# A graph convolution and mixture-of-experts kernel on one core: gather groups of eight, four and two blocks, and another order of the last stage

## The chip, the core and the metric

The kernel runs on one core of a Trainium2 chip, as one launch. The metric is the device time of that launch in microseconds (us). Engines are called by their short names: PE (TensorE), ACT (ScalarE), DVE (VectorE), POOL (GpSimd) and SP (SyncE, which only issues transfers here).

## What is computed

The input is x with 1250 rows of 1024, and 40000 edges, each with a source row, a target row and one of 8 types. Cut to what matters:

```python
xn = layernorm(x)
out = xn @ root + bias
for r in range(8):                       # mean over the edges of type r that end in a row
    sums = segment_sum(xn[src] * (type == r), dst);  cnt = segment_sum(type == r, dst)
    out += (sums / max(cnt, 1)) @ weight[r]
z = concat([out, xn]) @ w_gate + b_gate
x = x + tanh(out) * z + xn * (1 - z)
t = layernorm(x)                         # two of eight experts (1024 -> 512 -> 1024, relu) a row
x = x + layernorm(t + sum of the two experts' outputs, weighted) * gamma + beta
```

## The kernel before, in words

**Precision.** Every matmul operand is split in a rounded high part (made by ACT) and the rest, a low part (made by DVE); a product of 128 x 1024 by 1024 x 512 is three times eight matmuls. Weights come in chunks of four pieces of 128 x 1024: SP loads a piece (`load_piece`, L180), ACT makes its high part (`hi_piece`, L196), DVE its low part (`lo_piece`, L202). A raw buffer holds two pieces, so piece 2 of a chunk is only loaded when piece 0 has been split.

**Chunk stage.** The rows are first multiplied with all eight relation weights (16 chunks, ten row tiles each; PE line L211), and the products are stored in `y_dram`. One tile of one chunk is called a step here. Beside it, in chunks 1 to 3, the edges are sorted by target tile. Edge columns are taken four at a time (a batch, 79 in all): `hots` on DVE writes two one-hot tiles (L702, L705) into one of eight slots, and `counts` on PE multiplies them (L617), three batches at the end of each step, one step after the step in which DVE's list has them. PE waits there for `hot_ready`; DVE waits for `hot_used` of the batch eight before. The same DVE queue holds, at steps given in the table `side`, `starts` (where each tile's edges begin, L725 to L770), `positions` for ten tiles (L774 to L780: three tiles in step 2 of chunk 2, three in step 6, two in steps 0 and 2 of chunk 3), then `records`; and `lo_piece` in steps 2, 4, 6 and 8 of each chunk. Later POOL scatters 313 columns of records into the sorted list.

**Gather stage.** The sorted list has 332 blocks of 128 edges. For each block POOL gathers 128 rows of `y_dram` (512 KB) by an indirect DMA into one of eight slots (L982), ACT scales them into `y_hi`, which has two slots (L1030), DVE makes the low part (L1069), and PE adds both through a one-hot matrix into two PSUM banks: two matmuls for the high part (L1108), two for the low (L1115). ACT also makes the one-hot matrix (L993, L1002). Blocks that end in the same tile of target rows form a group: 78 groups of four and 10 groups of two. After each group DVE adds the two banks to `acc` (`flush`, L1051); it does so behind the low parts of the next group, and PE waits for the flush of the group two before. Two groups make a pass, 44 in all, numbered from 0. In each pass but four PE also works one unit, 24 matmuls of the products with root (the first 20 units, added to `acc` by DVE, also L1051) and with the gate weights (the next 20, copied by ACT, L1020); between the two matmul pairs of a block stand three of them. Passes 8, 19, 30 and 41 have no unit: in them the next chunk's four pieces are split, one ahead of each block, and their groups are short (two blocks each), as are those of pass 43. The pieces go into the buffer that the units before them read, so ACT waits for the last of these.

**Last stage.** Experts' outputs are scattered with addition into `sum_dram`. When the last is in, POOL adds `sum_dram` to `acc` by ten accumulating DMAs (L1710, one a tile). The tiles are normalised in groups (0 to 2, 3 to 5, 6 and 7, 8 and 9; L1832 to L1848 on DVE, L1786 on ACT). POOL adds tiles 0 to 7 to `out` by accumulating DMAs (L1714); for tiles 8 and 9 DVE adds rows that were loaded before (L1852) and SP stores them plainly (L1677).

## Time and profile before

| | us |
|---|---|
| median of 3 runs | 2188.13 |
| lowest and highest run | 2180.44, 2189.11 |
| the profiled execution | 2187.53 |
| its span in the trace | 2185.7 |
| chunk stage with the sort, about | 88 to 950 |
| gather stage | 960 to 1568 |
| last DMA landings | 2182 |

The terms are set against the profiled execution's 2187.53 us, which is 0.6 us under the median. Lines (L702) are those of the kernel before. The trace gives the start and the duration of each instruction; consecutive instructions of one engine can overlap by a little, so the distance of two starts is less than a duration where nothing lies between. Where the text says that a pass takes so long, it is from the first L1030 of its blocks to the first of the next pass.

### The profile page before, as it was taken

What the parts mean: (1) busy time and instruction counts of PE and PEld (TensorE: products, weight loads), DVE (VectorE), ACT (ScalarE), POOL (GpSimd) and SP (SyncE); (2) the same over time, 40 slices, a digit from 0 to 9 for tenths busy, and PEclk for the clock granted to TensorE, in tenths of its full rate; (3) what the DMA queues carried; (4) which work ended last, traced back from release to release, by engine and by line L of the source; (5) the groups of instructions that cost most, each with busy time, mean ns of one, the idle gap of its engine ahead of it and who ended that gap; (6) DMA issues with size and microseconds to landing.
All of it is one profiled execution on the core that took longest, in us unless ns stands there. A gap on an engine that the chain in (4) does not pass through costs nothing. (4 is left out here: it accounts for less than half of the span.)

```text
span 2185.7 us, 28064 instructions
## 1 busy us (share of the span) xinstructions
PE 2011.1 (92%) x9425; PEld 1596.2 (73%) x9425; DVE 1284.4 (59%) x2282; ACT 969.2 (44%) x1506; POOL 904.0 (41%) x801
## 2 busy tenths in 40 slices
PE   8999999999999999999899899899799579899970
PEld 6777778778888888877677577677488468788860
DVE  8589588832222222139899899899798742222215
ACT  3211122222222222249899799899644223233332
POOL 0000046565655555237677588688200022212212
PEclk9999999999999999999899899999799779999995
DMA  5224487777777877679889799899565579998439
GB/s 185 100 81 134 137 272 247 259 251 253 254 258 259 256 258 256 227 223 321 273 292 315 242 329 319 272 331 313 194 178 176 199 266 326 305 318 287 103 75 188
DMA packets 156848, 520.96 MB, mean 238 GB/s; under 512 B 30748, under 2 KB 31132, under 8 KB 154672
## 3 DMA queue, kind: packets, MB, share of 16 engines
q1 hardware_dynamic: 85616, 310.51, 41.1%
q0 software_dynamic: 71104, 208.84, 32.1%
q8 instruction: 68, 1.11, 0.2%
q14 instruction: 60, 0.49, 0.1%
HBM read 383.83 MB, written 154.68 MB: 246 GB/s over the span
## 5 line engine op out<-in xcount | busy, mean ns | idle before, releaser
L211 PE MATMUL psum<-w_hi,xnT_hi 128*128 128x512 f32 (+1 forms) x1592 | 421.1, 399 | 4.6 <-PEq L228 2.5
L211 PE MATMUL psum<-w_lo,xnT_hi 128*128 128x512 f32 (+1 forms) x1592 | 417.8, 393 | 0.0
L211 PE MATMUL psum<-w_hi,xnT_lo 128*128 128x512 f32 (+1 forms) x1592 | 413.7, 394 | 0.0
L882 POOL DMA_INDIRECT sorted_rows<-acc x313 | 342.9, 1096 | 116.7 <-issue 85.3
L580 ACT ACTIVATE work<-psum 128x512 f32<-128x512 f32 (+1 forms) x150 | 89.7, 598 | 661.5 <-PE psum L211 661.5
L211 PEld LDWEIGHTS psum<-w_hi,xnT_hi 128*128 128x128 f32 (+1 forms) x1592 | 293.5, 187 | 75.4 <-issue 4.0
L211 PEld LDWEIGHTS psum<-w_lo,xnT_hi 128*128 128x128 f32 (+1 forms) x1592 | 294.9, 185 | 73.2
L211 PEld LDWEIGHTS psum<-w_hi,xnT_lo 128*128 128x128 f32 (+1 forms) x1592 | 294.3, 185 | 71.1
L982 POOL DMA_INDIRECT w_hi<-y_rows,sort_row x168 | 221.2, 1317 | 78.3 <-PE psum L1115 41.3
L982 POOL DMA_INDIRECT w_lo<-y_rows,sort_row x164 | 217.9, 1329 | 77.2 <-PE psum L1115 38.6
L1108 PE MATMUL psum<-y_hi,hot 128*128 128x512 f32 x664 | 220.0, 414 | 30.2 <-ACT y_hi L1030 27.4
L1069 DVE SCALAR_TENSOR_TENSOR w_hi<-w_hi,sort_recip,y_hi 128x1024 fp32r<-128x1024 f32 x168 | 213.0, 1282 | 24.0 <-ACT y_hi L1030 19.0
L202 DVE TENSOR_TENSOR w_lo<-w_raw,w_hi 128x1024 fp32r<-128x1024 f32 x86 | 105.1, 1223 | 207.4 <-ACT w_hi L196 207.0
L1069 DVE SCALAR_TENSOR_TENSOR w_lo<-w_lo,sort_recip,y_hi 128x1024 fp32r<-128x1024 f32 x164 | 207.9, 1282 | 14.3 <-ACT y_hi L1030 9.1
L850 DVE TENSOR_TENSOR acc<-acc 128x1024 fp32r<-128x1024 f32 x64 | 78.4, 1225 | 220.0 <-ACT acc L589 220.0
L1030 ACT ACTIVATE y_hi<-w_hi,sort_recip 128x1024 fp32r<-128x1024 f32 x168 | 192.0, 1143 | 18.7 <-DVE w_hi L1069 8.5
L1030 ACT ACTIVATE y_hi<-w_lo,sort_recip 128x1024 fp32r<-128x1024 f32 x164 | 187.3, 1142 | 12.5 <-DVE w_lo L1069 8.7
L1108 PEld LDWEIGHTS psum<-y_hi,hot 128*128 128x128 f32 x664 | 124.9, 195 | 74.1 <-issue 35.3
L879 POOL TENSOR_TENSOR gate_word<-gate_word 1x1 f32<-1x1 f32 x40 | 8.4, 211 | 348.4 <-DVE acc L818 201.8
L1694 POOL DMA_INDIRECT sum_rows<-o_s,row_at x27 | 42.9, 1589 | 262.7 <-DMA sum_rows<-o_s,row_at 124.9
L993 ACT ACTIVATE apart<-lanes,sort_local 128x128 f16<-128x128 f32 x332 | 127.2, 386 | 6.1 <-DVE lanes L1044 6.1
L1051 DVE TENSOR_TENSOR acc<-acc,psum 128x1024 f32 (+2 forms) x108 | 120.6, 1117 | 2.5 <-DVE acc L1051 0.4
(334 smaller groups left out, 2614.0 us busy)
## 6 DMA issues: line engine op xcount, KB each, us to landing
split_experts<-acc SPq DMA_DIRECT2D x128, 512.0 KB, 4.2
ring<-split_experts SPq DMA_DIRECT2D x16, 4096.0 KB, 16.1
w_raw<-in_wchunks SPq DMA_DIRECT2D x86, 512.0 KB, 5.0
y_rows<-work SPq DMA_DIRECT2D x144, 256.0 KB, 2.8
acc<-in_wchunks SPq DMA_DIRECT2D x64, 512.0 KB, 6.0
work<-local_rows SPq DMA_DIRECT2D x26, 384.0 KB, 4.2
sum_rows<-work SPq DMA_DIRECT2D x22, 256.0 KB, 4.5
acc<-in_bias SPq DMA_DIRECT2D x10, 512.0 KB, 5.5
```

The costliest lines, as they stand in the source:

```text
L202: v.tensor_tensor(w_lo[:, s, q * PIECE:(q + 1) * PIECE], raw_piece(c, q), w_hi[:, s, q * PIECE:(q + 1) * PIECE].bitcast(F32), ALU.subtract)\
L211: i = pe.matmul(to[:rm, :], x_[:, k, m * P:m * P + rm], w_[:, s, k * HALF:(k + 1) * HALF], start=(n == 0), stop=(n == 3 * KD - 1))
L580: act.activation(stage_y[:rows(m), t % 4, :], bank[t % 4][:rows(m), :], ACT.Copy)\
L850: v.tensor_tensor(x_lo[:, p % 2, :], x_raw[:, p % 2, :], x_hi[:, p % 2, :].bitcast(F32), ALU.subtract).then_inc(x_lo_done, 1)
L882: pool.indirect_dma_start(sorted_dram, IndirectOffsetOnAxis(ap=e_dest[:, c:c + 1], axis=0), e_rec[:, c, :], None, bounds_check=BLOCKS * P ...
L982: pool.indirect_dma_start(slot_of(b).bitcast(F32), None, y_dram, IndirectOffsetOnAxis(ap=sort_row[:, COLUMN[j]:COLUMN[j] + 1], axis=0), bo ...
L993: act.activation(apart[:, k, :], lanes[:, :], ACT.Square, bias=sort_local[:, at:at + 1], scale=-1.0)\
L1030: act.activation(y_hi[:, j % 2, :], slot_of(b).bitcast(F32), ACT.Copy, scale=sort_recip[:, COLUMN[j]:COLUMN[j] + 1]).then_inc(hi_done, 1)
L1051: v.tensor_tensor(at, at, of, ALU.add).then_inc(acc_done, 1)
L1069: v.scalar_tensor_tensor(out=slot_of(b), in0=slot_of(b).bitcast(F32), scalar=sort_recip[:, COLUMN[j]:COLUMN[j] + 1], in1=y_hi[:, j % 2, :] ...
L1108: o = pe.matmul(bank[2 * h + q], hot[:, h, k, :], y_hi[:, j % 2, q * HALF:(q + 1) * HALF], start=first, stop=False)
L1694: pool.indirect_dma_start(sum_dram, IndirectOffsetOnAxis(ap=row_at[:, b:b + 1], axis=0), o_s[:, b % 2, :], None, compute_op=ALU.add).then_ ...
```

## The change

The list of groups has three kinds now: 34 groups of eight blocks (`LONG`), 10 of four and 10 of two, again 332 blocks. A group of eight fills both halves of a pass and one pair of banks, and is flushed once; the flushes fall from 88 to 54. Passes 8, 19, 30 and 41 have eight blocks; pieces 0 and 1 are split there ahead of the second block, piece 2 ahead of the seventh, piece 3 ahead of the eighth. Short passes (two and two blocks) are now 5, 11, 22, 33 and 43, passes with two groups of four are 4, 10, 21, 32 and 39; in a short pass with a unit six matmuls of it stand at each block.

In the sort, `starts` loses what comes behind the running sums; this goes into `shifts` (chunk 1, step 8) and `owners` (chunk 3, step 8). `positions` has one tile in each step from step 1 of chunk 2 to step 0 of chunk 3, and two more operations over 313 columns a tile.

In the last stage the order of tile groups is 8 and 9 first; SP loads their sums plainly into the ring of expert weights, DVE adds them, and DVE's last additions for these tiles stand behind the statistics of tiles 0 to 2. The core of the diff:

```diff
-SHORT = GROUP // 2
-SHORT_GROUPS = TILES
-LONG_GROUPS = -(-((EDGES + TILES * (SHORT * P - 1)) // (SHORT * P) - SHORT_GROUPS) // 4) * 2
-GROUPS = LONG_GROUPS + SHORT_GROUPS
+LONG, SHORT = 2 * GROUP, GROUP // 2
+SIDE_GROUPS = 2 * TILES
+LONG_GROUPS = -(-((EDGES + TILES * (SHORT * P - 1)) // (SHORT * P) - 3 * TILES) // 4)
+GROUPS = LONG_GROUPS + SIDE_GROUPS
+QUADS = 2 * LONG_GROUPS + SIDE_GROUPS
...
                     for t in range(1, TILES):
+                        v.tensor_tensor(t_mid_start[:, t:t + 1], t_mid_start[:, t - 1:t], t_mid[:, t - 1:t], ALU.add)
...
+                def shifts():
+                def owners():
...
                 def positions(first, last):
...
-                        link(v.tensor_scalar(e_tail, e_scan, t_tail[:, t:t + 1], t_shift[:, t:t + 1], ALU.is_gt, ALU.mult))
+                        v.tensor_scalar(e_tail, e_scan, t_mid_at[:, t:t + 1], t_mid_shift[:, t:t + 1], ALU.is_gt, ALU.mult)
+                        link(v.tensor_scalar(e_last, e_scan, t_odd_at[:, t:t + 1], t_odd_shift[:, t:t + 1], ALU.is_gt, ALU.mult))
                         link(v.tensor_tensor(e_scan, e_scan, e_tail, ALU.add))
+                        link(v.tensor_tensor(e_scan, e_scan, e_last, ALU.add))
...
-                side = {(HIST_CHUNK, 3): [turned], (HIST_CHUNK, 5): [starts],
-                        (HIST_CHUNK + 1, 2): [lambda: positions(0, 3)], (HIST_CHUNK + 1, 6): [lambda: positions(3, 6)],
-                        (HIST_CHUNK + 2, 0): [lambda: positions(6, 8)], (HIST_CHUNK + 2, 2): [lambda: positions(8, TILES)],
-                        (HIST_CHUNK + 2, 4): [records], (LOOK_CHUNK, 0): [table]}
+                side = {(HIST_CHUNK, 3): [turned], (HIST_CHUNK, 5): [starts], (HIST_CHUNK, 8): [shifts],
+                        (HIST_CHUNK + 2, 4): [records], (HIST_CHUNK + 2, 8): [owners], (LOOK_CHUNK, 0): [table]}
+                for t in range(TILES):
+                    side[(HIST_CHUNK + 1 + (t + 1) // TILES, (t + 1) % TILES)] = [lambda t=t: positions(t, t + 1)]
...
-        SHORT_PASSES = (*PIECES_AT, PASSES - 1)
+        SHORT_PASSES = (*(i + 3 for i in PIECES_AT if i + 3 < PASSES), TILES // 2, PASSES - 1)
+        MID_PASSES = (*(i - 1 for i in SHORT_PASSES[:-1]), PASSES - 5)
+        KIND = [SHORT if i in SHORT_PASSES else GROUP if i in MID_PASSES else LONG for i in range(PASSES)]
...
+        PIECES_BEFORE = {1: (0, 1), 6: (2,), 7: (3,)}
...
-                        if g >= 1:
+                        if g >= 1 and ENDS[g - 1]:
                             flush(g - 1)
...
-                        if g >= 2:
-                            pe.wait_ge(acc_done, ACC_NO[g - 2])
+                        if BEGINS[g] and PAIR[g] >= 2:
+                            pe.wait_ge(acc_done, ACC_NO[PAIR[g] - 2])
...
-                            for _ in itertools.islice(steps, 3 * KD // SLOTS):
+                            for _ in itertools.islice(steps, 3 * KD // (FIRST[2 * i + 2] - FIRST[2 * i])):
...
-            TAIL_GROUPS = ((0, 3), (3, 6), (6, 8), (8, 10))
+            TAIL_GROUPS = ((8, 10), (0, 3), (3, 6), (6, 8))
...
+                sp.wait_ge(o_added, 16 * BLOCKS_T)
+                for m in LAST_TILES:
+                    sp.dma_start(sum_here(m), sum_dram[m * P:m * P + rows(m), :]).then_inc(o_got[m], 16)
...
-                for m in range(TILES):
+                for m in range(LAST_TILES[0]):
                     pool.dma_start(acc[:rows(m), m, :], sum_dram[m * P:m * P + rows(m), :], accum_op=ALU.add)\
                         .then_inc(o_got[m], 16)
...
+                        if m in LAST_TILES:
+                            link(v.tensor_tensor(acc[:rm, m, :], acc[:rm, m, :], sum_here(m), ALU.add))
```

## Rows read from the trace of the kernel before

**Rows 1.** The page: span, and busy time of each engine.
```profile
span 2185.7 us, 28064 instructions
PE 2011.1 (92%) x9425; PEld 1596.2 (73%) x9425; DVE 1284.4 (59%) x2282; ACT 969.2 (44%) x1506; POOL 904.0 (41%) x801
```

**Rows 2.** Groups of DVE, 142.1 to 264.1: busy us, mean ns | idle before, releaser.
```profile
L702 DVE TENSOR_TENSOR acc<-acc 128x320 f16<-128x320 f32 (+1 forms) x53 | 25.5, 480 | 8.3 <-PE psum L617 8.1
L777 DVE TENSOR_TENSOR acc<-acc 128x313 f32<-128x313 f32 x10 | 4.9, 487 | 0.3
L776 DVE TENSOR_SCALAR acc<-acc 128x313 f32<-128x313 f32 x10 | 4.4, 442 | 0.4
```

**Rows 3.** Timeline in chunk 2: start, us, engine, line, [idle before <- releaser].
```profile
148.36 0.49 DVE L702 TENSOR_TENSOR acc<-acc 128x320 f16<-128x320 f32 x1 [3.01 <-PE psum L617]
148.77 0.69 DVE L705 TENSOR_TENSOR acc<-acc 128x512 f16<-128x512 f32 x1
...
160.21 0.63 PE L617 MATMUL psum<-acc 128*128 128x80 f16 x12
...
162.08 0.32 DVE L774 TENSOR_SCALAR acc<-acc 128x313 f32<-128x313 f32 x1
...
165.38 1.23 DVE L202 TENSOR_TENSOR w_lo<-w_raw,w_hi 128x1024 fp32r<-128x1024 f32 x1
166.52 0.48 DVE L702 TENSOR_TENSOR acc<-acc 128x320 f16<-128x320 f32 x1
...
167.53 0.48 DVE L702 TENSOR_TENSOR acc<-acc 128x320 f16<-128x320 f32 x1
```

**Rows 4.** Busy time by engine, ten steps of chunk 3 (columns as in rows 5).
```profile
203.10:264.10 61.00, 61.00 (x362) 48.12 (x359) 42.96 (x85) 9.78 (x15) 0.00 (x0) 1.00 0.39 125
```

**Rows 5.** Busy time: passes 12-16, 24-28, then 7-9, 18-20, 29-31, 40-42.
```profile
core 0: us, PE busy (x) PEld busy (x) DVE busy (x) ACT busy (x) POOL busy (x), PEclk, DMA share, GB/s
1132.40:1199.40 67.00, 65.98 (x281) 52.20 (x281) 64.41 (x56) 61.38 (x91) 51.57 (x40) 1.00 0.90 315
1299.10:1365.00 65.90, 65.90 (x282) 51.49 (x281) 61.42 (x51) 63.25 (x97) 53.64 (x41) 1.00 0.91 324
1061.10:1106.10 45.00, 37.30 (x129) 25.50 (x129) 38.25 (x34) 35.01 (x52) 28.17 (x22) 0.81 0.75 245
1212.80:1259.50 46.70, 37.65 (x129) 25.85 (x129) 38.38 (x34) 35.01 (x51) 26.54 (x20) 0.78 0.69 227
1365.00:1407.40 42.40, 34.07 (x129) 23.40 (x128) 36.41 (x31) 35.39 (x53) 26.12 (x20) 0.88 0.77 254
1513.30:1556.00 42.70, 32.85 (x107) 19.72 (x105) 35.67 (x31) 34.47 (x51) 25.45 (x19) 0.80 0.84 278
```

**Rows 6.** Timeline of DVE in pass 21: a flush and four low parts.
```profile
1266.89 1.22 DVE L1051 TENSOR_TENSOR acc<-acc,psum 128x1024 f32 x1
...
1268.03 5.21 DVE L1069 SCALAR_TENSOR_TENSOR w_lo<-w_lo,sort_recip,y_hi 128x1024 fp32r<-128x1024 f32 x4
```

**Rows 7.** The chain that ended last, one piece: 24 matmuls back to back.
```profile
1952.55 5.49 PE psum L1875 x24
```

**Rows 8.** Groups, 1212.8 to 1259.5 (passes 18 to 20).
```profile
L1108 PE MATMUL psum<-y_hi,hot 128*128 128x512 f32 x40 | 15.2, 465 | 7.7 <-ACT y_hi L1030 7.4 <-issue 0.2
L196 ACT ACTIVATE w_hi<-w_raw 128x1024 fp32r<-128x1024 f32 x4 | 4.2, 1054 | 8.0 <-DMA w_raw<-in_wchunks 5.6 <-PE psum L211 2.4
```

**Rows 9.** DMA, 2131 to 2183: busy tenths in 40 slices; queues: packets, MB, share.
```profile
DMA  7999999999999999999999999999999999998420
q0 software_dynamic: 2576, 9.32, 93.3%
q1 hardware_dynamic: 256, 0.93, 4.6%
```

**Rows 10.** Timeline of the end: POOL's last store, DVE's last addition.
```profile
2165.10 0.85 POOL L1714 DMA_DIRECT2D out<-acc  x1 [0.19 <-issue]
...
2171.39 1.22 DVE L1852 TENSOR_TENSOR acc<-acc,w_raw 98x1024 f32<-98x1024 f32 x1
```

More of the change, by code:

```diff
@@ L54 @@
 SLOTS = 8
-PASSES = GROUPS // 2
+PASSES = QUADS // 2
 UNITS = 4 * TILES
@@ L900, in program @@
                      4 * TILES + 1: CH_GATEU}
-        SHORT_PASSES = (*PIECES_AT, PASSES - 1)
-        ORDER, FIRST, COLUMN = [], [0], []
+        SHORT_PASSES = (*(i + 3 for i in PIECES_AT if i + 3 < PASSES), TILES // 2, PASSES - 1)
+        MID_PASSES = (*(i - 1 for i in SHORT_PASSES[:-1]), PASSES - 5)
+        assert not {*SHORT_PASSES, *MID_PASSES} & {*PIECES_AT}
+        KIND = [SHORT if i in SHORT_PASSES else GROUP if i in MID_PASSES else LONG for i in range(PASSES)]
+        BASE = {LONG: 0, GROUP: LONG_GROUPS * LONG, SHORT: LONG_GROUPS * LONG + TILES * GROUP}
+        NUMBER = {LONG: 0, GROUP: LONG_GROUPS, SHORT: LONG_GROUPS + TILES}
+        taken = {kind: 0 for kind in BASE}
+        OWNER, BEGINS, ENDS, PAIR, FIRST, COLUMN, pair = [], [], [], [], [0], [], -1
         for i in range(PASSES):
             for h in range(2):
-                short = i in SHORT_PASSES
-                n = sum((g >= LONG_GROUPS) == short for g in ORDER)
-                at, size = (LONG_GROUPS * GROUP + n * SHORT, SHORT) if short else (n * GROUP, GROUP)
-                ORDER.append(LONG_GROUPS + n if short else n)
-                COLUMN += range(at, at + size)
+                kind = KIND[i]
+                begins, ends = kind < LONG or h == 0, kind < LONG or h == 1
+                n, part = taken[kind], h * GROUP if kind == LONG else 0
+                pair += begins
+                OWNER.append(NUMBER[kind] + n)
+                BEGINS.append(begins)
+                ENDS.append(ends)
+                PAIR.append(pair)
+                at = BASE[kind] + n * kind + part
+                COLUMN += range(at, at + min(kind, GROUP))
                 FIRST.append(len(COLUMN))
+                taken[kind] += ends
         assert sorted(COLUMN) == list(range(BLOCKS))
@@ L916, in size_of, with pieces_in @@
             return FIRST[g + 1] - FIRST[g]
-        def pieces_in(i):
-            return [(PIECES_AT[i], q) for q in range(PIECES)] if i in PIECES_AT else []
+        PIECES_BEFORE = {1: (0, 1), 6: (2,), 7: (3,)}
+        def pieces_in(i, n=None):
+            if i not in PIECES_AT:
+                return []
+            return [(PIECES_AT[i], q) for q in (range(PIECES) if n is None else PIECES_BEFORE.get(n, ()))]
         def ended_before(i):
@@ L1021, in _ @@
                                         .then_inc(zx_read, 1)
-                        if pieces:
-                            c, q = pieces[n]
+                        for c, q in pieces_in(i, n):
                             act.wait_ge(mm_done, c * TILES)
@@ L1065, in _ @@
                             b = j % SLOTS
-                            if pieces:
-                                lo_piece(v, pieces[j - FIRST[2 * i]][0], 0, pieces[j - FIRST[2 * i]][1])
+                            for c, q in pieces_in(i, j - FIRST[2 * i]):
+                                lo_piece(v, c, 0, q)
                             v.wait_ge(hi_done, j + 1)
@@ L1114, in _ @@
                             for q in range(2):
-                                o = pe.matmul(bank[2 * h + q], hot[:, h, k, :], slot_of(b)[:, q * HALF:(q + 1) * HALF],
+                                o = pe.matmul(bank[two + q], hot[:, h, k, :], slot_of(b)[:, q * HALF:(q + 1) * HALF],
                                               start=False, stop=last)
@@ L1638, in program, with sum_here @@
             GOT = [p + 16 * len(range(i, BLOCKS, SLOTS)) for i, p in enumerate(PLACED)] + [0, 0]
-            TAIL_GROUPS = ((0, 3), (3, 6), (6, 8), (8, 10))
+            TAIL_GROUPS = ((8, 10), (0, 3), (3, 6), (6, 8))
+            TAIL_ORDER = [m for lo, hi in TAIL_GROUPS for m in range(lo, hi)]
             block = stage.enter_context(nc.Block())
             LAST = BLOCKS_T - 1
-            LAST_TILES = range(*TAIL_GROUPS[-1])
+            LAST_TILES = range(*TAIL_GROUPS[0])
             y_ready = ssem("f_y")
+            def sum_here(m):
+                return ring[:, 0, 0, 0, (m - LAST_TILES[0]) * D:(m - LAST_TILES[0] + 1) * D][:rows(m), :].bitcast(F32)
             def x1_rows(m):
@@ L1836, in _ @@
                         v.wait_ge(const_in, 16 * (1 + len(LAST_TILES)))
+                    if g == 1:
+                        for m in LAST_TILES:
+                            v.wait_ge(scaled, TAIL_ORDER.index(m) + 1)
+                            o = acc[:rows(m), m, :]
+                            v.tensor_tensor(o, o, x1_rows(m), ALU.add).then_inc(y_ready, 1)
                     s, std, r, w = var_of[:, lo:hi], std_of[:, lo:hi], recip_of[:, lo:hi], w_of[:, lo:hi]
```

113 lines of the change are left out of this document (69 added, 44 removed).

## The prediction

> **What bounds the kernel now.** I began with the page: PE is busy for 92% of the span and no other engine for over 59% [rows 1], so a change off PE pays only where PE waits for it, and costs only where it makes PE wait. The change touches three stages, and for each I asked for what ends last there.
>
> In the chunk stage PE does not pause at all: ten steps take 61.0 us, all of them PE's [rows 4], 6.1 a step. DVE has slack, but not much. It runs ahead in the one-hot batches until the eight slots stop it: it idles 3.01 us for PE's counts, then ends the third batch of a step at 149.46, and PE takes it at 160.5, in the burst from 160.21 [rows 3]. So DVE's lead is at most 11.0 us, and what it must do beyond 6.1 us a step is drawn from that.
>
> In the gather stage a pass takes 13.40 us in the root half and 13.18 in the gate half [rows 5]. In the first, DVE sets it: low parts are 1.30 apart and a flush takes 1.14 from start to start [rows 6]; eight of one, two of the other and one addition of a unit (0.72) make 13.4. In the second, PE is busy throughout [rows 5]. Its floor is 56 matmuls at 0.229 [rows 7], 12.8 us. The trios of passes around the four splittings are the poor stretches: 45.0, 46.7, 42.4 and 42.7 us, 176.8 in all, for 20 blocks each, at a mean clock of 0.78 to 0.88 [rows 5]. In one of them ACT waited 8.0 us ahead of the pieces, 5.6 for their loads and 2.4 for PE, and PE 7.7 for ACT [rows 8]. DMA engines are 90% busy in plain passes [rows 5].
>
> In the last stage the DMA engines are full from 2132 to 2178 [rows 9].
>
> **Chunk stage: `starts`, `positions`, `owners`.** A tile's positions take 3.30 us (162.08 to 165.38), a batch 1.01, a low piece 1.14 [rows 3]. Added to a tile are one comparison, 0.442 long and with nothing to wait for, so some 0.40, and one addition, 0.487 and a wait of 0.03 [rows 2]: 0.92, a tile 4.22. A step with one tile costs DVE 3.03 + 4.22 = 7.25 against PE's 6.1, so 1.13 is drawn ten times (11.3), and 1.14 for each of four low pieces (4.6): 15.9 against a lead of 11.0. **PE is starved for 4.9 us**, in the last three or four of these steps. The old order drew 9.9 + 1.14 + 3.03 - 6.1 = 8.0 at once for three tiles, and let the lead come back before the next three. Bounds: nothing, if the lead is full later than I think; 20, if PE's clock falls meanwhile (below). Of the rest, `starts` becomes shorter; `shifts`, a dozen small operations, falls where the lead can return; `owners`, some 46 of about 0.2, takes 9 us behind the last batches, where DVE idles 18 of 61 us [rows 4]: nothing. POOL and SP move no transfer here; the scatters start later by what PE loses.
>
> Weighed against the trace: a batch's two operations last 0.48 and 0.69 but the next batch starts 1.01 after [rows 3], so they overlap by 0.15. The Trainium skill ("VectorE: DVE Perf Modes", "The DRAIN you can't avoid") says that the next operation does not start until the pipeline has emptied; by that the batches cost 1.17, and the sum below would be worse by the 4.9 us that the second rival works out. The row decides; the rule is kept as that rival.
>
> **Gather stage, plain passes.** 34 flushes of 1.14 go, 39 us of DVE, but PE's floor catches most. Root half: DVE falls to 12.3, PE sets the pass with 12.8 and small waits, I take 12.97: 0.43 off each of nine passes (2, 3, 6, 12 to 17), 3.9. Gate half: 13.18 to 13.0 in eleven passes (23 to 28, 34 to 38), 2.0. Bounds: nothing, and 0.6 and 0.38 a pass at the bare floor. The second pass, where DVE still catches up, gives 0.5. Passes of two groups of four stay as they are.
>
> **Short passes with a unit.** Passes 5, 11, 22 and 33 have 40 matmuls, 9.2 us at the floor, I take 9.4, where plain passes stood: 4.0 off twice and 3.8 twice, **15.6 off**. This is no gain yet: the four blocks taken out stand in the splitting passes.
>
> **Splitting passes, now eight blocks.** ACT gives PE one more block before it waits, and five blocks lie between pieces 1 and 2 in which these land, so most of the 8.0 of wait is filled. What is late next is DMA: eight gathers and four pieces, twelve times 0.524 MB, 6.3 MB; at the 324 GB/s and 0.91 of [rows 5] the engines give 356 full, so 17.7 us. DVE has 8 x 1.30 + 4 x 1.14 + 1.14 = 16.1 and some waits. I take 18.2, and 18.8 with the gate half's stores. The pass ahead takes 12.97 or 13.0; the one behind 13.2 and 1.5 for a low clock (bounds 0 and 6), in the third region 14.0 in all, and 12.2 behind the last, which has no unit. The trios: 45.9, 45.9, 45.8 and 44.0, together 181.6 against 176.8, **4.8 more**, for 24 blocks each instead of 20. Bounds: 10 less to 8 more.
>
> Gather stage in all: 3.9 + 2.0 + 0.5 + 15.6 - 4.8 = **17.2 off**, bounds 5 and 30. Waits for the flush two groups back go, and none comes in their place: a flush now stands half a pass behind its group.
>
> **Last stage.** POOL's queue took 93.3% of 52 us for 9.32 MB, 5.2 us a MB; SP's 4.6% for 0.93 MB, 2.6 a MB [rows 9]. Two tiles (0.93 MB) that go from accumulating to plain save 2.4 us of a full resource. Against it, DVE has two additions of 1.22 more [rows 10], and the accumulating stores, which cost most, now end the kernel: for tiles 6 and 7 they were issued by 2165.1, 6 us ahead of DVE's last addition [rows 10], and now are last in DVE's order. I take **1.5 off**, bounds 2.4 off and 3 more. The Trainium skill ("DMA: Bandwidth & Descriptors", "Issuing engines are not separate DMA queues") says that another issuing engine saves only the time of issue; by that alone the move would give under 1 us. The rows above price the accumulation, not the issuer.
>
> **Sum.** 2187.5 + 4.9 - 17.2 - 1.5 = 2173.7; the profiled execution lies 0.6 under the median, so **2174 us**. About 0.5%, 11 us, is what a measurement of this kernel can tell from no change; the border to faster lies at 2177.
>
> **Rivals.**
> 1. *PE's clock falls when DVE starves it in chunk 2 and 3* (slower). In the trios PE's pauses came with a mean clock of 0.78 to 0.88 [rows 5]. A step's 24 matmuls at 1.2 GHz instead of 2.4 cost 5.5 more. Over four starved steps 22, which takes the place of the 4.9: 2174 + 17 = 2191. It decides from the point where over three steps run low; five give 2196, six over 2199. For it: DVE stays the slower engine in these steps, so pauses repeat. Against it: a slow PE lets DVE catch up, which ends the pauses. Chance 0.13.
> 2. *DVE's operations cost their full durations*: batches 1.17, so 0.48 more a step over ten steps, 4.9 more, 2179. Against it, [rows 3]. Chance 0.07.
> 3. *Transfers bind the gather stage.* Passes stay at 13.4 and 13.18 because landings come later, and the splitting passes take 20: 5.9 and 8 less gain, partly made up in the passes behind: 2184. For it, 0.90 and 0.91 [rows 5]; against it, a plain pass would need only 0.94 of the engines. Chance 0.18.
> 4. *No starvation*: 2169. Chance 0.08.
>
> **How the numbers follow.** The forecast has 0.54, from 2166 to 2182 by its own terms, 0.44 of it faster and 0.10 the same. Rival 1 gives 0.08 slower and 0.05 the same; rival 2 mostly the same (0.06); rival 3 0.15 the same, 0.01 faster, 0.02 slower; rival 4 faster. The rest of rival 2 is faster. That makes 0.54 faster, 0.36 the same, 0.10 slower. The range reaches from the low end of rival 4 to rival 1's value: 2161 to 2190.
>
> **What would show it.** In the changed trace: waits of L617's line for DVE's one-hot tiles of some 5 us, in the last steps of chunk 2 and the first of chunk 3, clock at 1.00 there; 54 full flushes; plain passes of 12.9 to 13.0 with DVE under 95%; short passes of 9.4; splitting passes of 18 to 19 with ACT's wait for pieces under 2 us each; the last landing 1 to 2 us nearer to the last scatter. The prediction is wrong if PE never waits in the chunk stage or waits over 10 us, if plain passes do not shorten, or if the trios cost over 190 us.

## The result and the profile after

The kernel after takes 2175.53 us in the median of 8 runs (2168.59 to 2178.73), the kernel before 2188.73 beside it (8 runs, 2180.44 to 2194.39): a ratio of 0.9943, interval 0.9926 to 0.9960. That is 13.2 us faster by the medians and 12.5 us by the ratio. The forecast was 2174. Medians hide how it came about, so the profiled execution (2178.36 us, span 2176.6) is cut where stages meet, beside before's and a later execution of the same kernel after (e10):

| us | before | after | e10 |
|---|---|---|---|
| start to the first block scaled (L1030, after L1080) | 966.0 | 977.5 | 975.3 |
| gather stage, to the last block scaled | 595.9 | 569.7 | 572.5 |
| to the landing of the last scatter into `sum_dram` | 567.2 | 572.9 | 567.9 |
| to the kernel's last landing | 52.9 | 52.9 | 51.6 |
| to the end of the span | 3.7 | 3.6 | 3.6 |

The page after, with what answers to [rows 1]:

```profile
span 2176.6 us, 27961 instructions
PE 2012.9 (92%) x9425; PEld 1601.7 (74%) x9425; DVE 1263.6 (58%) x2307; ACT 970.8 (45%) x1506; POOL 913.2 (42%) x799
```

PE is as busy as before in a span 9.1 us shorter: nothing was taken from its work.

**Chunk stage.** The groups of DVE from 149.9 to 279.5 answer to [rows 2]; L810 and L811 are the comparisons, L812 and L813 the additions:

```profile
L706 DVE TENSOR_TENSOR acc<-acc 128x320 f16<-128x320 f32 (+1 forms) x50 | 24.0, 480 | 6.9 <-PE psum L621 6.7
L812 DVE TENSOR_TENSOR acc<-acc 128x313 f32<-128x313 f32 x10 | 4.9, 487 | 0.3
L813 DVE TENSOR_TENSOR acc<-acc 128x313 f32<-128x313 f32 x10 | 4.9, 487 | 0.3
L810 DVE TENSOR_SCALAR acc<-acc 128x313 f32<-128x313 f32 x10 | 4.4, 443 | 0.4
L811 DVE TENSOR_SCALAR acc<-acc 128x313 f32<-128x313 f32 x10 | 4.4, 437 | 0.0
```

The timeline where chunk 2 meets chunk 3 answers to [rows 3]:

```profile
203.80 0.48 DVE L706 TENSOR_TENSOR acc<-acc 128x320 f16<-128x320 f32 x1
204.20 0.68 DVE L709 TENSOR_TENSOR acc<-acc 128x512 f16<-128x512 f32 x1
...
204.67 0.63 PE L621 MATMUL psum<-acc 128*128 128x80 f16 x12
204.81 0.32 DVE L808 TENSOR_SCALAR acc<-acc 128x313 f32<-128x313 f32 x1
...
208.46 0.48 DVE L816 TENSOR_TENSOR acc<-acc 128x313 f32<-128x313 f32 x1
208.98 1.23 DVE L203 TENSOR_TENSOR w_lo<-w_raw,w_hi 128x1024 fp32r<-128x1024 f32 x1
...
210.30 3.75 PE L212 MATMUL psum<-w_hi,xnT_hi 128*128 128x512 f32 x8 [5.00 <-issue]
```

The seventh tile's positions are done, and the eighth's (L808 to L816) begin. PE ends its 12 counting matmuls at 205.3 and stands still until 210.30. It waits for the last low piece of chunk 3's weights (L203), which is in DVE's queue behind these positions. The wait is called "issue" because the releaser is not resolved; the low piece ends at 210.21 and PE starts 0.09 later. The eight matmuls behind it take 3.75 us. The windows, with the columns of [rows 5], show the clock:

```profile
203.10:209.30 6.20, 2.20 (x20) 1.43 (x18) 5.96 (x13) 0.60 (x1) 0.00 (x0) 1.00 0.00 0
209.30:216.20 6.90, 5.90 (x14) 4.67 (x15) 6.73 (x13) 0.00 (x0) 0.00 (x0) 0.51 0.65 214
```

0.51 is the lower level, 1.2 GHz. From the start of one step's counts to the start of the next, this one step takes 13.96 us instead of 6.11: 5.0 of wait and 2.8 for matmuls at the low clock. All others of chunks 2 and 3 take what they took, so 7.85 of the 11.5 us by which the stage is longer are here (7.5 of 9.3 in e10).

Another 2.3 us lie where the sort's counting has ended and the forecast had nothing. From the fourth step of chunk 4 (283.86 before, 293.05 after) to the first block scaled (966.01, 977.54) it is 682.1 us before and in e1, and 684.2 to 684.6 in all twelve traces of kernels with the new groups: a step of 24 matmuls takes 5.57 us there instead of 5.55, over some 118 steps in which PE hardly pauses. Which part of the program does this was not tested. What is left is mostly in the first 100 us, which differ between executions (the fourth step of chunk 1 starts at 97.6 to 100.9, whatever the kernel).

**Gather stage.** Windows of passes 13 to 17 and 24 to 28, then the trios 7 to 9, 18 to 20, 29 to 31 and 40 to 42 (24 blocks each now, 20 before), against [rows 5]:

```profile
1145.20:1210.10 64.90, 64.90 (x281) 52.49 (x281) 59.09 (x51) 61.81 (x91) 51.67 (x40) 1.00 0.91 323
1288.50:1354.40 65.90, 65.90 (x282) 51.81 (x281) 56.18 (x46) 63.20 (x96) 53.13 (x41) 1.00 0.94 337
1065.70:1110.10 44.40, 37.91 (x146) 26.63 (x145) 40.09 (x35) 41.16 (x60) 35.04 (x26) 0.96 0.93 334
1210.10:1253.30 43.20, 38.08 (x148) 27.04 (x147) 40.02 (x35) 40.54 (x60) 33.54 (x24) 0.96 0.95 344
1354.40:1398.00 43.60, 38.97 (x147) 27.50 (x146) 38.22 (x32) 41.39 (x61) 34.44 (x25) 0.92 0.96 349
1499.20:1541.50 42.30, 35.58 (x125) 22.92 (x123) 38.33 (x33) 40.61 (x60) 34.34 (x24) 0.92 0.97 352
```

A root pass now takes 12.99 and all of it is PE. A gate pass takes 13.18 as before, and a second look at [rows 5] shows why: PE was busy for 65.90 of 65.90 us there too, with 5.2 us of DVE work more. The trios take 173.3 us for 96 blocks, where they took 176.8 for 80, at a mean clock of 0.92 to 0.96 instead of 0.78 to 0.88. In the first splitting pass the groups of ACT and DVE that answer to [rows 8] read:

```profile
L203 DVE TENSOR_TENSOR w_lo<-w_raw,w_hi 128x1024 fp32r<-128x1024 f32 x4 | 4.8, 1223 | 1.4 <-ACT w_hi L197 1.4
L197 ACT ACTIVATE w_hi<-w_raw 128x1024 fp32r<-128x1024 f32 x4 | 4.1, 1056 | 1.5 <-DMA w_raw<-in_wchunks 1.0 <-PE psum L212 0.4
```

ACT's wait ahead of the pieces is 1.5 us, 1.0 of it for loads, where in the same pass before it was 6.3 and 3.9; in passes 19, 30 and 41 it is 0.4, 0.0 and 0.0 ([rows 8] has 8.0 before for pass 19). Windows of the four splitting passes, then the 3.7 us behind the first of them, and the DMA view of the first:

```profile
1078.70:1096.50 17.80, 11.89 (x40) 6.19 (x38) 16.20 (x15) 16.17 (x24) 14.43 (x11) 1.00 0.97 355
1223.20:1240.30 17.10, 12.69 (x40) 7.60 (x38) 16.05 (x15) 16.01 (x23) 12.82 (x9) 0.90 0.95 339
1367.60:1385.10 17.50, 13.48 (x40) 8.34 (x38) 15.59 (x14) 16.72 (x24) 13.89 (x9) 0.80 0.96 343
1512.40:1529.30 16.90, 12.72 (x40) 7.36 (x38) 15.18 (x14) 16.37 (x24) 14.08 (x8) 0.90 0.95 342
1096.50:1100.20 3.70, 3.12 (x7) 2.44 (x8) 3.64 (x4) 3.69 (x6) 2.51 (x2) 0.54 1.02 410
```

```profile
DMA packets 1727, 6.31 MB, mean 355 GB/s; under 512 B 187, under 2 KB 187, under 8 KB 1726
```

They take 17.79, 17.14, 17.51 and 16.95 us, the passes behind them 13.44, 12.97, 12.93 and 12.14 (pass 42 has no unit, nor has 43; with the four that the description names there are six). The low clock has not gone: it holds for 3.4 us right behind the first splitting pass, and for part of each of the others. A short pass and the one behind it take 22.65 (root) and 22.95 (gate) together.

**Last stage.** The last 53 us, before and then after (the first fence is before's):

```profile
2129.10:2182.00 52.90, 0.00 (x0) 0.00 (x0) 32.58 (x66) 11.63 (x14) 15.91 (x18) 0.50 0.96 194
```

```profile
2120.10:2173.00 52.90, 0.00 (x0) 0.00 (x0) 34.92 (x68) 11.62 (x14) 14.03 (x16) 0.50 0.95 194
```

DVE has 2.34 us more, and nothing is gained. What the DMA engines had to do, share of the engines times the stretch, comes to 50.9 us before (91.7% for POOL's 9.32 MB and 4.5% for SP's 0.93 MB) and 50.1 us after (packets, MB, share of the engines):

```profile
q0 software_dynamic: 2304, 8.39, 84.2%
q1 hardware_dynamic: 512, 1.85, 10.5%
```

POOL's stores wait for ACT's scaling of each group of tiles and go out later than they did: the last (2163.72, below) 43.6 us behind the last scatter's landing, where it was 36.0 before. L1902 are DVE's last additions for tiles 8 and 9.

```profile
2138.64 1.22 DVE L1902 TENSOR_TENSOR acc<-acc,t_s 128x1024 f32<-128x1024 f32 x1
2139.78 1.22 DVE L1902 TENSOR_TENSOR acc<-acc,w_raw 98x1024 f32<-98x1024 f32 x1
...
2147.00 0.87 POOL L1773 DMA_DIRECT2D out<-acc  x1 [19.16 <-ACT acc L1845]
...
2156.23 0.84 POOL L1773 DMA_DIRECT2D out<-acc  x1 [6.29 <-ACT acc L1845]
...
2162.68 0.86 POOL L1773 DMA_DIRECT2D out<-acc  x1 [3.53 <-ACT acc L1845]
2163.72 0.84 POOL L1773 DMA_DIRECT2D out<-acc  x1 [0.18 <-issue]
```

### The profile page after: what moved, and what is told of

Same layout as the page of the kernel before. It is cut to its first block and busy times, and to the rows that moved or that the text cites. A ratio compares the mean times of both kernels' runs of the same rounds, so it can differ in the third digit from the quotient of the medians.

```text
span 2176.6 us, 27961 instructions
## 1 busy us (share of the span) xinstructions
PE 2012.9 (92%) x9425; PEld 1601.7 (74%) x9425; DVE 1263.6 (58%) x2307; ACT 970.8 (45%) x1506; POOL 913.2 (42%) x799
## 3 DMA queue, kind: packets, MB, share of 16 engines
q1 hardware_dynamic: 85872, 311.44, 41.3%
## 5 line engine op out<-in xcount | busy, mean ns | idle before, releaser
L1034 POOL DMA_INDIRECT w_hi<-y_rows,sort_row x168 | 230.8, 1374 | 63.2 <-issue 38.0
L1159 PE MATMUL psum<-y_hi,hot 128*128 128x512 f32 x664 | 214.2, 404 | 11.2 <-ACT y_hi L1080 10.6
L203 DVE TENSOR_TENSOR w_lo<-w_raw,w_hi 128x1024 fp32r<-128x1024 f32 x86 | 104.8, 1224 | 189.7 <-ACT w_hi L197 188.8
L1080 ACT ACTIVATE y_hi<-w_hi,sort_recip 128x1024 fp32r<-128x1024 f32 x168 | 192.1, 1144 | 14.7 <-DMA w_hi<-y_rows,sort_row 6.0
L1080 ACT ACTIVATE y_hi<-w_lo,sort_recip 128x1024 fp32r<-128x1024 f32 x164 | 187.6, 1144 | 10.2 <-issue 2.8
L1159 PEld LDWEIGHTS psum<-y_hi,hot 128*128 128x128 f32 x664 | 125.2, 192 | 49.5 <-ACT y_hi L1080 16.2
L1166 PE MATMUL psum<-w_hi,hot 128*128 128x512 f32 x336 | 112.0, 415 | 7.2 <-DVE w_hi L1119 7.1
```

The lines of the kernel that those rows point to most:

```text
L203: v.tensor_tensor(w_lo[:, s, q * PIECE:(q + 1) * PIECE], raw_piece(c, q), w_hi[:, s, q * PIECE:(q + 1) * PIECE].bitcast(F32), ALU.subtract)\
L1034: pool.indirect_dma_start(slot_of(b).bitcast(F32), None, y_dram, IndirectOffsetOnAxis(ap=sort_row[:, COLUMN[j]:COLUMN[j] + 1], axis=0), bo ...
L1080: act.activation(y_hi[:, j % 2, :], slot_of(b).bitcast(F32), ACT.Copy, scale=sort_recip[:, COLUMN[j]:COLUMN[j] + 1]).then_inc(hi_done, 1)
L1159: o = pe.matmul(bank[two + q], hot[:, h, k, :], y_hi[:, j % 2, q * HALF:(q + 1) * HALF], start=first, stop=False)
L1166: o = pe.matmul(bank[two + q], hot[:, h, k, :], slot_of(b)[:, q * HALF:(q + 1) * HALF], start=False, stop=last)
```

## The experiments

All medians; every ratio is to runs of the kernel before on the same chip. "First block" is the first L1080 (L1030), "gather" from there to the last, "last stage" from the last scatter's landing to the last landing of the kernel, all of the profiled execution.

| | median us (runs) | ratio, interval | first block | gather | last stage |
|---|---|---|---|---|---|
| before | 2188.73 (8) | | 966.0 | 595.9 | 52.9 |
| after | 2175.53 (8) | 0.9943, 0.9926 to 0.9960 | 977.5 | 569.7 | 52.9 |
| e1 sort alone | 2196.36 (8) | 1.0041, 1.0025 to 1.0057 | 972.6 | 594.0 | 53.4 |
| e2 sort spread | 2167.19 (6) | 0.9912, 0.9895 to 0.9928 | 967.0 | 570.5 | 51.2 |
| e3 piece first | 2174.35 (6) | 0.9936, 0.9918 to 0.9954 | 974.4 | 574.1 | 54.4 |
| e4 flush length | 2179.43 (11) | 0.9963, 0.9950 to 0.9977 | 975.6 | 576.0 | 52.1 |
| e5 pieces together | 2197.15 (7) | 1.0038, 1.0021 to 1.0056 | 977.1 | 593.4 | 51.1 |
| e6 additions last | 2176.72 (6) | 0.9941, 0.9926 to 0.9955 | 975.0 | 572.3 | 53.9 |
| e7 old last stage | 2172.80 (6) | 0.9932, 0.9909 to 0.9955 | 975.6 | 569.1 | 53.1 |
| e8 spread, additions last | 2164.24 (5) | 0.9887, 0.9870 to 0.9904 | 967.6 | 570.9 | 52.9 |
| e9 groups alone | 2191.06 (12) | 1.0019, 1.0001 to 1.0038 | 975.2 | 591.3 | 51.8 |
| e10 after again | 2172.03 (6) | 0.9943, 0.9921 to 0.9965 | 975.3 | 572.5 | 51.6 |
| e11 spread, old last stage | 2166.70 (6) | 0.9917, 0.9895 to 0.9939 | 968.2 | 571.4 | 53.0 |
| e12 pieces 2 and 3 early | 2199.88 (4) | 1.0062, 1.0042 to 1.0082 | 975.2 | 596.1 | 50.9 |

### What the sort costs, and why

**e1_sort_alone** is the kernel before with the table of steps of the kernel after and two more operations a tile, whose results are not used:

```diff
-                side = {..., (HIST_CHUNK + 1, 2): [lambda: positions(0, 3)], (HIST_CHUNK + 1, 6): [lambda: positions(3, 6)],
-                        (HIST_CHUNK + 2, 0): [lambda: positions(6, 8)], (HIST_CHUNK + 2, 2): [lambda: positions(8, TILES)], ...}
+                for t in range(TILES):
+                    side[(HIST_CHUNK + 1 + (t + 1) // TILES, (t + 1) % TILES)] = [lambda t=t: positions(t, t + 1)]
...
+                        link(v.tensor_scalar(e_last, e_scan, t_tail[:, t:t + 1], t_shift[:, t:t + 1], ALU.is_gt, ALU.mult))
...
+                        link(v.tensor_tensor(e_last, e_last, e_tail, ALU.add))
```

> The kernel before with one part of the change: positions for one tile in each step from chunk 2 step 1 on, and two more DVE operations a tile (their results are not used). Gather and last stage stay as before. Theory A (at the start of chunk 3 PE waits for the last low weight piece, which stands in DVE's queue behind the positions; PE then runs its first matmuls at half clock): one step of about 14 us instead of 6.1, total 8 us above before, about 2197. Theory B (the prediction's: PE is starved for one-hot tiles in three or four steps): 5 us above, 2194, spread over steps, with the waits at the count matmuls. Theory C (the sort costs nothing, the 8 us of the changed trace come from elsewhere): 2189.

Measured: 9.1 us above before, and the same long step, here of 14.02 us:

```profile
205.92 1.22 DVE L202 TENSOR_TENSOR w_lo<-w_raw,w_hi 128x1024 fp32r<-128x1024 f32 x1
...
207.25 3.75 PE L211 MATMUL psum<-w_hi,xnT_hi 128*128 128x512 f32 x8 [5.03 <-issue]
```

The sort's new place and length, without any of the groups, make the long step. The slower plain steps are not in e1: its first block is scaled 6.6 us later than before's, with 7.9 more in the long step.

**e2_spread** is the kernel after with the tiles' positions drawn out, over steps counted from the first of chunk 1 (`records` goes to step 6 of chunk 3):

```diff
-                for t in range(TILES):
-                    side[(HIST_CHUNK + 1 + (t + 1) // TILES, (t + 1) % TILES)] = [lambda t=t: positions(t, t + 1)]
+                for t, at in enumerate((10, 11, 12, 13, 15, 17, 19, 21, 23, 25)):
+                    side[(HIST_CHUNK + at // TILES, at % TILES)] = [lambda t=t: positions(t, t + 1)]
```

> The changed kernel with the ten positions spread over steps 0, 1, 2, 3, 5, 7 and 9 of chunk 2 and 1, 3, 5 of chunk 3, and the records in step 6 of chunk 3: every step with positions is followed by one that lets DVE's lead return, and none stands ahead of the last low piece of chunk 3. Theories A and B: no step over 6.2 us, lead never under 5 us, 8 us below the changed kernel, about 2167.5. Theory C: no difference, 2175.5. If the scatters, which start later by two steps' records at most, were on the path, it would come back there: 2175.

Measured: 2167.19. No step there is over 6.12 us, and the stretch of the long step is full:

```profile
205.00:227.00 22.00, 22.00 (x135) 17.51 (x134) 20.57 (x41) 3.31 (x6) 0.00 (x0) 1.00 0.33 106
```

The same work on DVE costs nothing when its lead is never used up.

**e3_piece_first** puts that low piece ahead of the positions in the one step where it was late:

```diff
+                            if (c, m) == (HIST_CHUNK + 1, 8):
+                                lo_piece(v, c + 1, 1 - s, m // 2 - 1)
                             for of in side.get((c, m), ()):
                                 of()
...
```

> The changed kernel with the last low piece of chunk 3 ahead of the positions in step 8 of chunk 2, nothing else. Theory A alone (only the piece is late): the long step goes from 14 to about 7 us, the others stay at 6.1, 7 us below the changed kernel, 2168.5. Theories A and B together (with the piece out of the way PE next waits for one-hot tiles): the same DVE work is still too much for the lead, three or four steps of 6.5 to 8 us, in all 4 us of wait instead of 8, total 4 us below, 2171.5.

Measured: 2174.35. The long step is gone and four steps of 7.14 to 7.32 us stand in its place, 4.4 us in all, with one-hot tiles late as the prediction had them:

```profile
205.12 1.22 DVE L203 TENSOR_TENSOR w_lo<-w_raw,w_hi 128x1024 fp32r<-128x1024 f32 x1
...
206.44 2.10 PE L212 MATMUL psum<-w_hi,xnT_hi 128*128 128x512 f32 x8 [0.86 <-issue]
...
213.60 0.32 PE L621 MATMUL psum<-acc 128*128 128x80 f16 x4 [0.68 <-DVE acc L709]
```

```profile
205.10:233.90 28.80, 25.62 (x148) 19.74 (x145) 28.07 (x55) 3.33 (x5) 0.00 (x0) 1.00 0.31 104
```

PE pauses for 3.2 of these 28.8 us at a clock of 1.00. The median can't be told from that of the kernel after; the trace can: 3.4 us less in steps there.

### Where the gather stage's gain comes from

**e4_flush_length** gives DVE two linked multiplications that write a scratch tile, about 1.15 us, behind the low parts of each group of eight, where the kernel before had the flush of its first four blocks:

```diff
                         if g >= 1 and ENDS[g - 1]:
                             flush(g - 1)
+                        elif g >= 1:
+                            v.wait_ge(pe_done, FIRST[g])
+                            for _ in range(2):
+                                link(v.tensor_tensor(idle, ..., ALU.mult))
```

> The changed kernel with DVE work of a flush's length (about 1.15 us, on a scratch tile, after the same wait as a flush) where the old kernel had the flushes that now are gone; PE does not wait for it. Theory A (fewer flushes gain through DVE's time in the root half and little in the gate half): root passes back from 13.0 to 13.4, gate passes unchanged at 13.2, the passes that split pieces, where DVE is 91% busy, up by 1.1 each: 9 times 0.4 and 4.5, about 8 us above the changed kernel, 2183.5. Theory B (the gain came from PE no longer waiting for banks, not from DVE's time): under 2 us above, 2177.

Measured: 2179.43; the gather stage is 6.3 us longer (3.5 than in e10). Passes 13 to 17 and 24 to 28:

```profile
1144.70:1211.10 66.40, 66.30 (x282) 52.18 (x281) 63.87 (x61) 61.33 (x91) 50.81 (x40) 1.00 0.91 317
1291.20:1357.10 65.90, 65.90 (x282) 51.75 (x281) 61.46 (x56) 63.13 (x96) 49.37 (x40) 1.00 0.95 338
```

Root passes rise by 0.29 us (of the 0.41 that they had lost), gate passes not at all, so DVE's time counts only where DVE had set the pass. Most of the 26 us must have another source.

**e9_groups_alone** has the new groups in the old places: the splitting passes are short again, with a piece ahead of each of their four blocks.

```diff
-        SHORT_PASSES = (*(i + 3 for i in PIECES_AT if i + 3 < PASSES), TILES // 2, PASSES - 1)
-        MID_PASSES = (*(i - 1 for i in SHORT_PASSES[:-1]), PASSES - 5)
+        SHORT_PASSES = (*PIECES_AT, PASSES - 1)
+        MID_PASSES = (4, 10, 21, 32, 39)
...
-        PIECES_BEFORE = {1: (0, 1), 6: (2,), 7: (3,)}
+        PIECES_BEFORE = {0: (0,), 1: (1,), 2: (2,), 3: (3,)}
```

> The kernel after with groups of eight, four and two, but the places of the kernel before: passes 8, 19, 30 and 41 are short again (four blocks, one piece ahead of each), so no short pass has a unit except the last; passes 4, 10, 21, 32 and 39 have groups of four. Theory A (fewer flushes are worth only what the root passes lose, 0.41 us each, as e4_flush_length said; the rest of the gather stage's 26 us comes from four more blocks beside the pieces): about 13 root passes at 13.0 instead of 13.4 and one at 0.6 less, gate passes at 13.18 as ever, trios at 175 to 177 us for 20 blocks each, the gather stage 589 to 592 us (before 595.9, after 569.7), and the median, which has the sort's 8 to 10 us on it, 2190 to 2196. Theory B (the flushes are the main thing): the gather stage below 580 and the median 2177 to 2183.

Measured: gather 591.3 us, median 2191.06. Fewer flushes alone bring 4.6 of the 26 us; with the sort's cost on top this kernel is not faster than before. Its trios 7 to 9 and 18 to 20 are like those of [rows 5]:

```profile
1068.00:1112.80 44.80, 36.59 (x130) 25.38 (x129) 36.09 (x32) 34.97 (x52) 29.71 (x21) 0.81 0.74 245
1217.10:1262.90 45.80, 35.90 (x130) 24.99 (x129) 36.05 (x32) 34.94 (x52) 27.56 (x20) 0.85 0.70 230
```

**e5_pieces_together** is the kernel after with eight blocks in the splitting passes, but the pieces ahead of the first four; **e12_half_way** leaves pieces 0 and 1 in the place of the kernel after.

```diff
-        PIECES_BEFORE = {1: (0, 1), 6: (2,), 7: (3,)}
+        PIECES_BEFORE = {0: (0,), 1: (1,), 2: (2,), 3: (3,)}      e5
+        PIECES_BEFORE = {1: (0, 1), 2: (2,), 3: (3,)}             e12
```

> The kernel after, with pieces 0, 1, 2 and 3 split ahead of blocks 0, 1, 2 and 3 of passes 8, 19, 30 and 41 instead of ahead of blocks 1, 1, 6 and 7. Theory A (the gather stage owes its gain beyond the shorter DVE queue to the place of the pieces: the load of piece 2, which can only start when piece 0 has been split, lies beside six blocks): ACT waits for the loads of pieces 2 and 3 with nothing else to do, each of the four passes takes 20 to 23 us instead of 17.0 to 17.8, and the median is 12 to 20 us above that of the kernel after (2175.5), about 2191. Theory B (these passes are bound by the bytes they move, 6.3 MB, wherever the pieces stand): the four passes stay at 17 to 18 us and the median at 2175 to 2178.

> The kernel after with pieces 0 and 1 where it has them (ahead of block 1) and pieces 2 and 3 ahead of blocks 2 and 3 instead of 7 and 8. It splits the 22 us that e5_pieces_together lost into the wait of piece 0 for PE's last unit and the wait of pieces 2 and 3 for their loads. Theory A (both count: in e5_pieces_together the pass ahead took 15.85 instead of 13.02, the splitting passes 20.2 to 21.9 instead of 17.0 to 17.8, the pass behind 0.5 to 1 less): the pass ahead is back at 13.0, the splitting passes take 20 to 21 and those behind 12.3, so trios of 45.5 to 47, 183 to 187 us in all (after 173.3), the gather stage about 582 and the median about 2186. Theory B (the loads are all of it): trios of 48 to 49, the gather stage above 590. Theory C (piece 0's wait for PE is all of it): trios of 43 to 44 and a gather stage of 570 to 573.

Measured: 2197.15 and 2199.88, gather stages of 593.4 and 596.1 us. The trios take 195.6 us in e5 (48.3, 48.3, 49.6, 49.3) and 199.1 in e12 (48.7, 49.3, 50.6, 50.4), against 173.3 after. ACT's timelines, first e5:

```profile
1080.66 1.06 ACT L197 ACTIVATE w_hi<-w_raw 128x1024 fp32r<-128x1024 f32 x1 [1.76 <-PE psum L212]
...
1089.53 1.06 ACT L197 ACTIVATE w_hi<-w_raw 128x1024 fp32r<-128x1024 f32 x1 [4.20 <-DMA w_raw<-in_wchunks]
```

then e12:

```profile
1077.94 2.01 ACT L197 ACTIVATE w_hi<-w_raw 128x1024 fp32r<-128x1024 f32 x2 [0.43 <-PE psum L212]
...
1087.82 1.06 ACT L197 ACTIVATE w_hi<-w_raw 128x1024 fp32r<-128x1024 f32 x1 [6.55 <-DMA w_raw<-in_wchunks]
```

and the kernel after:

```profile
1080.55 2.01 ACT L197 ACTIVATE w_hi<-w_raw 128x1024 fp32r<-128x1024 f32 x2 [0.43 <-PE psum L212]
...
1090.85 1.06 ACT L197 ACTIVATE w_hi<-w_raw 128x1024 fp32r<-128x1024 f32 x1 [0.77 <-DMA w_raw<-in_wchunks]
```

From the start of piece 0's split to the start of piece 2's it is 8.9, 9.9 and 10.3 us: the load that piece 0 lets go takes that long in a full gather stage, wherever the pieces stand. What differs is what ACT has to do meanwhile: two blocks in e5, one in e12, five in the kernel after. My theory of e12, that piece 0's wait for PE had a large part in e5's loss, was wrong; e12 was to win back 10 us and lost 3 more (its theory B). And the clock comes on top: over the first splitting pass it is 1.00 after, and in e12

```profile
1076.10:1099.50 23.40, 13.05 (x40) 7.29 (x38) 16.30 (x15) 16.12 (x23) 12.65 (x9) 0.78 0.89 313
```

The low clock comes with the longer waits here; no run separates what each costs. So four more blocks in a splitting pass and pieces 2 and 3 at its end are worth 19 to 22 us together (591.3 in e9 to 572.5 in e10 and 569.7), and the first without the second loses 2 to 5 (593.4, 596.1).

### The last stage and the stretch before it

**e6_adds_last** moves the loop of DVE's last additions behind the last group's statistics, **e7_old_last_stage** takes the whole last stage of the kernel before into the kernel after, **e8_spread_adds_last** and **e11_spread_old_last_stage** do the same to e2_spread, and **e10_after_again** is the kernel after, unchanged. The edit of e6 and e8:

```diff
-                    if g == 1:
-                        for m in LAST_TILES:
-                            v.wait_ge(scaled, TAIL_ORDER.index(m) + 1)
...
+                for m in LAST_TILES:
+                    v.wait_ge(scaled, TAIL_ORDER.index(m) + 1)
```

and the core of that of e7 and e11:

```diff
-            TAIL_GROUPS = ((8, 10), (0, 3), (3, 6), (6, 8))
+            TAIL_GROUPS = ((0, 3), (3, 6), (6, 8), (8, 10))
...
-                for m in range(LAST_TILES[0]):
+                for m in range(TILES):
                     pool.dma_start(acc[:rows(m), m, :], sum_dram[...], accum_op=ALU.add)
```

> The kernel after, with DVE's two last additions (tiles 8 and 9, 1.14 us each) put behind the statistics of the last group instead of behind those of the second. Theory A (DVE's queue sets when the last tiles are normalised and these two additions stand in its way): the stores of tiles 3 to 7 go out up to 2.3 us earlier and the distance from the last scatter's landing to the last landing of the kernel falls from 56.5 to 54 to 55 us; median 2173 to 2174. Theory B (the accumulating DMAs set the end by their bytes): the distance stays at 56.5 within 0.5 us and the median at 2175.5.

> The kernel after with the last stage of the kernel before (ten accumulating DMAs from POOL, tile groups in their old order). Theory A (the new last stage brings nothing, as the equal distances of 56.6 and 56.5 us in the two traces say): the distance is 56.6 within 0.5 us and the median that of the kernel after within 1 us. Theory B (the new last stage is worth what the forecast gave it): 58 us and a median 1.5 us above that of the kernel after, about 2177.

> The kernel of e2_spread (positions of the tiles drawn out over chunks 2 to 4, so that DVE's lead is never used up) and the edit of e6_adds_last together. If the two are independent, as they should be with 1800 us between them: the median of e2_spread (2167.2) less what e6_adds_last gives, that is 2165 to 2166 by theory A of e6_adds_last and 2167 by its theory B; no step of chunks 2 to 4 longer than 6.9 us, and passes as in the kernel after.

> The kernel after, unchanged, for the scatter of its stages. Theory A (the 5.7 us by which the kernel after lost between the last block gathered and the last scatter's landing is scatter of one execution): this stretch takes 566.5 to 571.7 us here, as in the other traces, instead of 572.9, the gather stage 568 to 572, and the last stage 51 to 54.5 from the last scatter's landing to the last landing. Theory B (something of the change slows the expert stage): 572 to 574 again.

> The kernel of e2_spread with the last stage of the kernel before. Theory A (no arrangement of the last stage tried is worth anything that can be told): median 2164 to 2167, like e2_spread (2167.2) and e8_spread_adds_last (2164.2), and 52.5 to 53.5 us from the last scatter's landing to the last landing. Theory B (the new last stage is worth 1.5 us): 2167 to 2169.

(The 56.5 and 56.6 us in these texts were counted to the end of the span, 3.5 to 3.7 behind the last landing; the table counts to the landing.) Measured: with the old last stage it takes 52.9, 53.4, 53.1 and 53.0 us (before, e1, e7, e11), with the new one 50.9 to 54.4, 52.0 in the mean of eight (after, e2 to e5, e9, e10, e12), and with the additions moved 53.9 and 52.9. The new stage may be worth 1 us (53.1 less 52.0), which is less than its own scatter. The DMA engines' work says the same with less scatter: 50.9 to 51.3 us in the four traces of the old stage, 49.5 to 50.7 in these eight of the new one. e6's theory A, 2 us to be had from the order of DVE's queue, is not borne out: the last store goes out at 41.3 and 40.6 us behind the scatter (e6, e8) instead of 42.6 to 44.0, and lands no sooner. The medians of e2, e8 and e11 (2167.2, 2164.2, 2166.7) have overlapping intervals.

The stretch between the gather stage and the last scatter takes 567.9 us in e10, and 566.5 to 571.9 in all other traces but that of the kernel after, 572.9. The 5.7 us that this one execution seemed to lose there are scatter between executions.

## Why the prediction was right, and where it was not

The time was right: 2174 forecast, 2175.53 measured (2172.03 for e10). None of its three terms was, and it is luck that they made up for one another: the chunk stage cost more than forecast, the gather stage gave more, and the last stage gave less.

- **Chunk stage, forecast 4.9 more, measured 7.85 in one step, and 9.3 to 11.5 for the stage.** The ledger held: a tile's positions take 4.17 us from 204.81 to 208.98 (forecast 4.22), and the lead, 11.1 us at its fullest, is down to some 0.1 at 204.67, when seven of the ten tiles and three of the four low pieces are drawn from it (7 x 1.13 + 3 x 1.14 = 11.3). The step that failed is "PE is starved for 4.9 us, in the last three or four of these steps", for one-hot tiles. In the same queue stood a low piece that PE needs at a fixed point, the first step of chunk 3. With the lead gone, PE waits at once for all that DVE has ahead of it, one tile's positions and the piece itself (208.98 + 1.23 - 204.81 = 5.4, less the 0.5 us of counting): 5.00 us, as much as the forecast's 4.9 by chance. One wait of 5 us, and not four of 1, then brought the low clock, 2.8 us more. This is rival 1's mechanism, but once and not over four steps. e3, with the piece out of the way, shows the forecast as it stood: 4.4 us over four steps, clock 1.00. The 2.3 us in plain steps are a term that the forecast did not have, and their cause is open.
- **Rival 2** (operations at full duration) fell: 0.40 lies between the two operations of a batch (203.80 and 204.20; the first is called 0.48), as in [rows 3]. By the Trainium skill ("VectorE: DVE Perf Modes", "The DRAIN you can't avoid") the next operation waits until the pipeline has emptied; the rows do not bear that out here. The same section adds that "A next op that is not held starts earlier", which the prediction left out and which agrees with the 0.40.
- **Gather stage, forecast 17.2 off, measured 26.2 (23.4 in e10).** By terms, before to after: root passes 2, 3 and 13 to 17 give 2.9 (forecast 3.0). Passes 0 and 1 give 1.0 (0.5). The passes around the short ones (4 to 6, 10 to 12, 21 to 23, 32 to 34) go from 159.2 to 141.1, 18.1 off (15.6 and 1.2 of plain passes). The ten gate passes 24 to 28 and 35 to 39 give 0.4 where 1.6 was set for nine of them: "13.18 to 13.0" failed. PE was already busy without a gap in [rows 5], and a floor taken from the expert stage [rows 7] is not the pace of this one; e4 put the work back on DVE and the pass stayed at 13.18.
- **Trios, forecast 181.6, measured 173.3 and 175.8 (e10).** This is the term that failed most, within its bounds. Bytes and rate were right: 6.31 MB at 355 GB/s in the first splitting pass, which took 17.79 against "17.7, I take 18.2". In the other three 339 to 343 GB/s over 16.95 to 17.51 us come to 5.8 to 6.0 MB, so part of the traffic lies in the passes beside them, and 18.2 and 18.8 were 4.6 too high in sum. The other half, 4.1 us, is in the passes behind, for the first three of which I had set 14.0 to 14.7, 1.5 us of it for a low clock: they took 12.93 to 13.44. The low clock came (0.50 to 0.54, for 3.4 to 6.9 us a trio) but fell behind the splitting only in the first and in part in the fourth; otherwise it lay within a splitting pass, where the DMA engines were busy for 91% and more meanwhile. That it cost little there because transfers set the pace fits the rows and was not tested.
- **Rival 3** (transfers bind) did not come about in plain passes, and is now next: DMA share 0.91 to 0.97 in all stretches of its gather stage shown above.
- **Last stage, forecast 1.5 off, measured nothing to 1.1.** The step that failed is the price, "save 2.4 us of a full resource": the DMA engines had 50.9 us of work before and 50.1 after (50.2 in e10). The two tiles took 4.0 us out of POOL's queue (48.5 to 44.5) and put 3.2 into SP's (2.4 to 5.6), not 4.8 and 2.4: a mean of 5.2 or 2.6 us a MB was not the price of this MB. The other half of the sum was off as well. "The accumulating stores ... now end the kernel" was no news, since the last landing that the trace of before shows is that of POOL's last store too (2165.1 to 2182.0). The new order sends that store 7.6 us later and it lands no later, so the time of its issue alone does not set the end. By the Trainium skill ("DMA: Bandwidth & Descriptors", "Issuing engines are not separate DMA queues") another issuing engine saves only the time of issue, and the prediction's estimate from that was under 1 us; the 0 to 1.1 us measured do not contradict it, but no run separates the issuer from the accumulation.
- What would have shown it wrong: PE did not wait over 10 us in the chunk stage, the root passes shortened, the trios stayed under 190. The look at L617's line would have shown nothing, though, since the wait stood at the products' line.

**The better version.** e2 (2167.2) beats both kernels, and e8, with the same sort, has the lowest median, 2164.24, ratio 0.9887 (0.9870 to 0.9904), 24 us under before. What makes it is the sort's table; e8's other edit brought nothing that can be told.

## What to carry to other kernels

When side work is put into a queue that runs ahead of a bound engine, keep a ledger of the lead, and then ask of every instruction in that queue when its reader needs it: the first with a fixed due time takes the whole shortage at once, and one long pause costs the clock as well. When work is merged, count first what the merged thing cost where the bound engine stood: 39 us of DVE's flushes were worth some 3 to 6 (e9, e4). A load that is released late is best covered by placing its use as late as the order allows; here the same blocks and pieces in another order make the difference between a gain of 23 to 26 us and next to none. And where a forecast of several terms comes true, look at each term before trusting the sum.
